# Scaling graph messages with the attention weight: 25 ScalarE activations per chunk for one VectorE product

## The chip, the cores and the metric

The kernel runs on one core of a Trainium2 chip. The metric is the device time of one execution in microseconds (us); the time before is the median of three runs. One further execution was recorded by the hardware profiler, and every duration below comes from it. PE is TensorE, DVE VectorE, ACT ScalarE, POOL GpSimd, SP the engine that issues most plain loads.

## What is computed

One graph attention layer over 12,500 nodes and 400,000 edges that are sorted by destination:

```python
xl = einsum('ni,nio->no', h, hetero_w[node_type]) + hetero_b[node_type]      # h = relu(layernorm(x))
alpha = lrelu(concat([xl[dst], xl[src], ete, eae]) @ att_w)                  # one score per edge
alpha = exp(alpha - amax[dst]);  alpha = alpha / (segment_sum(alpha, dst) + 1e-16)
msg = concat([xl[src], eae]) @ lin_w * alpha                                 # 32 numbers per edge
out = x + segment_sum(msg, dst)
```

The product `... * alpha` in the fourth line is what the change is about. The kernel does not know the final maximum and denominator while it passes over the edges; it multiplies each message by exp(score minus the running maximum) and carries 32 sums and the denominator along.

## The kernel before

**Tiling.** Each of the 128 partitions owns 3125 consecutive edges, cut into 125 chunks of T = 25 edges. A loop of 25 iterations holds 5 chunks each (u = 0 to 4, each with its own input buffers; the last iteration is written out after the loop). The message of an edge (before scaling) is a row of a node table gathered by source node plus a PE product of the edge attributes.

**Gathers.** POOL issues an indirect DMA for each column of 128 edges: 21, 22, 21, 22 and 21 per chunk in the five chunks (`gath[u]`, line 443), 2675 in all. The 3 or 4 remaining columns of a chunk are made by PE and DVE with one-hot products (lines 636, 949, 970, 976). POOL waits only for a chunk's index buffer `meta_sb[u]`, which SP reloads once the scan of the chunk five before is over. So POOL can run up to five chunks ahead.

**Order in one chunk.** DVE makes the picks of destination scores (line 983) and the one-hots (949, 997), then waits for the chunk's gathers and adds them to PE's product (lines 1048 and 1050, into `msg`). It works out the score, the running maximum and the exponents' arguments (to line 1072, `args_ready`). ACT makes the exponential (533, `exp_done`), copies two columns to the output rows (536, 537), and spreads the decay factors (540, `keep_ready`). DVE meanwhile copies the last sums (1078), the weights (1086) and makes the product of messages and weights (1087) into `terms`. `terms` is stored as 33 fields by 26 edge places, so that the scan along the edges (1094) can run over all fields in one instruction: consecutive fields of an edge lie 26 numbers apart. The scan needs `terms` and `keep`. After it ACT copies the sums to the output rows (546), issues their store, and begins the 50 sign activations of the next chunk (526, 528), which feed a count on PE (691). ACT then waits for the next arguments. `nc.scalar.mul` in `scale_attr` (518) is an activation too and already stands between exponential and signs in each chunk.

The chunk bodies of each engine are plain instruction sequences; counters (semaphores) order them across engines. `need(k, at)` and `step` are waits and increments of DVE's own counter.

Of the kernel before, what the change touches and what calls it, by code (L numbers as in the profile page):

```python
# [7 lines left out]
F_IN = 32  # L8
# [6 lines left out]
P = 128  # L15
# [3 lines left out]
T = 25  # L19
# [27 lines left out]
def gnn_kernel(nc, x, meta, dst_rows, dst_tmajor, sel_src, row_edges, row_last, edge_attr_t, node_type,  # L47
               hetero_wT, hetero_bT, edge_type_emb, edge_attr_w, att_w, lin_w, out):
    fp32, bf16, i32 = mybir.dt.float32, mybir.dt.bfloat16, mybir.dt.int32
    ALU, ACT, AX = mybir.AluOpType, mybir.ActivationFunctionType, mybir.AxisListType  # L50
# [13 lines left out]
    with ctx:  # L64
        def sb(name, shape, dt=fp32):
            return ctx.enter_context(nc.sbuf_tensor(name, shape, dt))

        def sem(name):
            return ctx.enter_context(nc.semaphore(name))
# [36 lines left out]
        def in_node_buf(at, shape, parts=P):  # L106

            size = shape[0] * shape[1]
            return node_buf[0:parts, at:at + size].rearrange("p (a b) -> p a b", b=shape[1])
# [36 lines left out]
        msg = in_node_buf(2 * TG * P, [T, VW])  # L146
# [3 lines left out]
        wts = sb("wts", [P, 2, T])  # L150
        terms = in_node_buf(2 * TG * P + T * VW, [VW, T + 1])
# [14 lines left out]
        def part_of(k, g):  # L166
            return parts[:, k, g, :].rearrange("p (f n) -> p f n", n=GN)
# [23 lines left out]
        scale = sb("scale", [P, 2, NPP])  # L191
# [79 lines left out]
        args_ready = sem("args_ready")  # L271
        exp_done = sem("exp_done")
        keep_ready = sem("keep_ready")
        sums_ready = sem("sums_ready")
        rows_sums = sem("rows_sums")
        head_idx_ready = sem("head_idx_ready")
# [37 lines left out]
        def count(n):  # L314

            return n + 1

        def selected(i, u):

            return i * TS_ITER + TS_BEFORE[u]  # L320

        def start_at_one(eng, *sems):
            for s in sems:
                eng.sem_inc(s, 1)

        def is_unsorted(eng):
            eng.wait_ge(unsorted_ready, 1)
            return eng.value_load(unsorted_i[0:1, 0:1], min_val=0, max_val=1)
# [153 lines left out]
        @block.scalar  # L482
        def _(act):
            start_at_one(act, hmT_sb, rows_sums, *stored)

            act.wait_ge(node_w_mm, 1)
            nc.scalar.copy(node_w[:], ps_misc[:, 0, 0:YW])
            nc.scalar.copy(node_b[:], ps_misc[0:MB, 0, YW:2 * YW]).then_inc(node_w_sb, 1)
            act.wait_ge(var_ready, 1)
            nc.scalar.sqrt(stat[:, 3, :], stat[:, 2, :]).then_inc(dev_ready, 1)  # L490
            with act.Fori(0, NODE_ITERS // 2) as i:
                for k in range(2):
                    n = i * 2 + k
                    act.wait_ge(hmT_mm, n + 1)
                    act.wait_ge(tab_mm, n + 1)
                    for b, w in enumerate((4 * P, 3 * P)):
                        last = nc.scalar.copy(hmT[k][:, b * 4 * P:b * 4 * P + w], ps_hmT[k][:, b, 0:w])
                    last.then_inc(hmT_sb, 1)

            act.wait_ge(tab_sb, NODE_ITERS + 2)  # L500
            for g in range(NG):
                nc.scalar.copy(part_of(0, g), table_group[g]).then_inc(part_copied, 1)
            for g in range(NG):
                act.wait_ge(rest_ready, g + 1)
                nc.scalar.copy(part_of(1, g), part_rest[g]).then_inc(part_copied, 1)
            for g in range(NG):
                act.wait_ge(rest_ready, NG + g + 1)
                last = nc.scalar.copy(part_of(2, g), part_rest[g])
            last.then_inc(parts_ready, 1)
            act.wait_ge(parts_ready, 1)  # L510
            act.wait_ge(head_counted, 1)
            act.wait_ge(table_out, 16)

            def scale_attr(c):

                act.wait_ge(attr_mm, c + 1)
                act.wait_ge(eae_ready, count(c))
                nc.scalar.mul(eae_s, ps_attr[0:G * F_EDGE, :, 0:TG * P // 2], SLOPE).then_inc(eae_scaled, 1)

            def chunk(i, u, final):  # L520
                c = i * U + u

                act.wait_ge(places_ready, c + 1)
                act.wait_ge(signs_mm, count(c))
                for t in range(T):
                    nc.scalar.activation(sign_hi[:, t, :], half128[:], ACT.Sign, bias=hic[u][:, t:t + 1],  # L526
                                         scale=-1.0)
                    last = nc.scalar.activation(sign_lo[:, t, :], half128[:, 0:NPP], ACT.Sign,  # L528
                                                bias=loc[u][:, t:t + 1], scale=-1.0)
                last.then_inc(signs_ready, 1)  # L530

                act.wait_ge(args_ready, c + 1)
                nc.scalar.activation(wts[:], args[:], ACT.Exp).then_inc(exp_done, 1)  # L533

                act.wait_ge(stored[u], i * 16 + 1)
                nc.scalar.copy(rows[u][:, :, VW], mrun[:, 1:T + 1])
                nc.scalar.copy(rows[u][:, :, VW + 1], dstc[u][:, 1:T + 1])
                act.wait_ge(exp_done, c + 1)
                act.wait_ge(sums_ready, count(c))
                nc.scalar.copy(keep[:, :, 1:T + 1], wts[:, 1:2, :].broadcast_to([P, VW, T])).then_inc(  # L540
                    keep_ready, 1)
                if not final:
                    scale_attr(c + 1)

                act.wait_ge(sums_ready, count(c + 1))
                nc.scalar.copy(rows[u][:, :, 0:VW], sums[:, :, 1:T + 1].rearrange("p f t -> p t f")).then_inc(  # L546
                    rows_sums, 1)
                act.wait_ge(rows_sums, count(c + 1))
                act.dma_start(rows_pm[:, ds(c * T, T), :], rows[u][:]).then_inc(stored[u], 16)

            scale_attr(0)
            with act.Fori(0, ITERS - 1) as i:
                for u in range(U):
                    chunk(i, u, False)
            for u in range(U):
                chunk(ITERS - 1, u, u == U - 1)

            flag = is_unsorted(act)
            with act.If(flag < 1):
                act.wait_ge(targs_ready, 1)  # L560
                nc.scalar.activation(wtail[:], mtail[:], ACT.Exp)
                nc.scalar.activation(fix[:, 2:3], fix[:, 1:2], ACT.Exp).then_inc(texp_done, 1)
            with act.If(flag >= 1):
                with act.Fori(0, EPP) as t:
                    act.wait_ge(merge_args, t + 1)
                    nc.scalar.activation(wtail[:], mtail[:], ACT.Exp)
                    nc.scalar.activation(fix[:, 2:3], fix[:, 1:2], ACT.Exp).then_inc(merge_exp, 1)
# [169 lines left out]
        def _(dve):  # L737
            v = nc.vector
# [11 lines left out]
            def step(ins):  # L750

                steps[0] += 1
                ins.then_inc(dve_step, 1)
                return steps[0]
# [218 lines left out]
            def take_sum(i, u, j):  # L973

                dve.wait_ge(sel_read, count(selected(i, u) + j + 1))
                return step(v.tensor_reduce(gath[u][:, T - 1 - j, 0:VW], sel_prod, AX.X, ALU.add))  # L976
# [23 lines left out]
            def chunk(i, u, at, final):  # L1000
                c = i * U + u
# [54 lines left out]
                k = step(v.tensor_tensor(alpha[:], msg[:, :, F_IN], escore[:], ALU.add))  # L1056
# [3 lines left out]
                k = step(v.scalar_tensor_tensor(alpha[:], alpha[:], SLOPE, alpha[:], ALU.mult, ALU.max))  # L1060
# [4 lines left out]
                k = step(v.tensor_tensor_scan(mrun[:, 1:T + 1], pen[:], alpha[:], mrun[:, 0:1], ALU.add, ALU.max))  # L1065
# [3 lines left out]
                k = step(v.tensor_tensor(args[:, 1, :], mrun[:, 0:T], pen[:], ALU.add))  # L1069
# [13 lines left out]
                if not final:  # L1083
                    place(3, *after, at)
                dve.wait_ge(exp_done, c + 1)
                v.tensor_copy(terms[:, F_IN, 1:T + 1], wts[:, 0, :])
                k = step(v.tensor_tensor(terms[:, 0:F_IN, 1:T + 1].rearrange("p f t -> p t f"), msg[:, :, 0:F_IN],  # L1087
                                         wts[:, 0, :].unsqueeze(2).broadcast_to([P, T, F_IN]), ALU.mult))
                if not final:
                    k_take = take_sum(*after, 2)  # L1090
                dve.wait_ge(keep_ready, c + 1)
                dve.wait_ge(rows_sums, count(c))
                need(k, at)
# [19 lines left out]
            with dve.Fori(0, ITERS - 1) as i:  # L1113
                for u in range(U):
                    chunk(i, u, i * STEPS, False)
            assert steps[0] == before + STEPS
            steps[0] = before + STEPS * (ITERS - 1)
            for u in range(U):
                chunk(ITERS - 1, u, 0, u == U - 1)
# [160 lines left out]
```

## Time and profile before

| | |
|---|---|
| median of the runs | 5777.1 us (5774.23 to 5807.59) |
| profiled execution, first to last instruction | 4081.6 us |
| VectorE busy in it | 2835.9 us |
| ScalarE busy in it | 2278.0 us |
| GpSimd busy in it | 3109.5 us |
| chunk loops, about | 160 to 3920 us of it |

The profiled execution's span is 1695.5 us shorter than the median of the runs; the profile shows nothing of what lies around the span. Times inside the span are read from the trace, times of the whole kernel from the runs. "Idle before" of a group is the time in which the engine stood still directly ahead of that group's instructions, with what it waited for; "issue" means that no other engine's work is seen as the cause.

### The profile page before, as it was taken

Reading aid. Unit: us, or ns where it says so; the run is one execution under the profiler, and the core shown is the slowest. Engines: PE = TensorE matmul, PEld = TensorE weight load, DVE = VectorE, ACT = ScalarE, POOL = GpSimd, SP = SyncE. Lnnn points to the kernel's source line nnn. Section 1 sums busy time; section 2 is a strip of 40 time slices with the busy share of each in tenths; the row PEclk is TensorE's granted clock in tenths of the full one; section 3 lists DMA queues with packets and bytes.
Section 4 is the critical chain, followed back from the end, with each engine's and each line's share of the span. In section 5 each row is a group of like instructions: output and inputs, shape, how many; then the busy total and the mean of one; then the engine's idle time right before and its main releaser. Section 6 shows DMA issues by size and latency. Waiting matters only on the chain.

```text
span 4081.6 us, 79224 instructions
## 1 busy us (share of the span) xinstructions
PE 3088.9 (76%) x24063; PEld 1924.5 (47%) x24063; DVE 2835.9 (69%) x12580; ACT 2278.0 (56%) x7080; POOL 3109.5 (76%) x2790
## 2 busy tenths in 40 slices
PE   5787877787787877887878877777877887887820
PEld 4454544444444544544544444444544554554510
DVE  6887776776776776776776776776776776776730
ACT  2466565565565565565565565565565565665620
POOL 1777777777777777777777777777777777777757
PEclk9899889888889898888898898999998889989865
DMA  3932232232232232232232232232232332322211
GB/s 99 103 76 64 62 78 62 62 79 62 62 79 62 63 78 62 63 78 62 62 78 62 63 78 62 62 79 62 65 76 62 69 73 62 77 64 62 43 35 29
DMA packets 188948, 273.63 MB, mean 67 GB/s; under 512 B 84416, under 2 KB 145232, under 8 KB 187616
## 3 DMA queue, kind: packets, MB, share of 16 engines
q1 hardware_dynamic: 81584, 162.45, 15.5%
q0 software_dynamic: 88800, 48.54, 10.5%
q10 hardware_dynamic: 18000, 56.01, 3.5%
q8 instruction: 246, 4.03, 0.4%
q14 instruction: 318, 2.61, 0.2%
HBM read 204.76 MB, written 62.01 MB: 65 GB/s over the span
## 4 chain that ended last, share of the span: by engine, by line
POOL 75%; issue 21%; PE 1%; DMA 1%; DVE 1%; SPq 0%; POOLq 0%; ACT 0%; ACTq 0%; DVEq 0%
POOL gath L443 73%; POOL node_buf L478 2%; PE ps_misc L603 1%; PE ps_misc L600 0%; DMA tails<-rows_dram 0%; DMA table_dram<-node_buf 0%; DMA rlast_i<-row_last_in 0%; PE ps_pick L612 0%; PE ps_attr L591 0%; DMA rows_dram<-rows 0%; DMA gath<-table_dram,meta 0%; PE ps_pick L591 0%; DVE sums L1094 0%; SPq L356 0%; ACT rows L546 0%
## 5 line engine op out<-in xcount | busy, mean ns | idle before, releaser
L443 POOL DMA_INDIRECT gath<-table_dram,meta x2675 | 3009.7, 1125 | 904.8 <-issue 904.5
L636 PE MATMUL ps_misc<-parts,dst_f 128*128 128x462 bf16 x9450 | 2011.1, 372 | 9.7 <-issue 6.4
L636 PEld LDWEIGHTS ps_misc<-parts,dst_f 128*128 128x128 bf16 x9450 | 935.1, 101 | 958.4 <-issue 147.6
L526 ACT ACTIVATE hi_f<-half,hic 128x128 bf16<-128x128 f32 x3125 | 1209.2, 387 | 61.7 <-ACT rows L546 61.4
L528 ACT ACTIVATE hi_f<-half,loc 128x98 bf16<-128x98 f32 x3125 | 1130.1, 362 | 0.0
L983 DVE SCALAR_TENSOR_TENSOR h<-free,loc,ps_pick 128x98 f32<-128x98 f32 x3125 | 778.6, 308 | 87.7 <-issue 87.0
L648 PE MATMUL ps_pick<-s_dst,onehot 128*128 128x98 bf16 x9375 | 539.0, 215 | 210.7 <-DVE h L983 151.1
L691 PE MATMUL ps_msg<-hi_f 128*128 128x98 bf16 x3125 | 244.0, 261 | 545.1 <-DVE node_buf L1050 545.1
L1048 DVE TENSOR_TENSOR node_buf<-gath,ps_msg 128x495 f32<-128x495 f32 x125 | 83.5, 668 | 818.6 <-DMA gath<-table_dram,meta 818.6
L648 PEld LDWEIGHTS ps_pick<-s_dst,onehot 128*128 128x128 bf16 x9375 | 485.6, 102 | 299.7 <-DVE h L983 193.5
L533 ACT ACTIVATE wts<-args 128x50 f32<-128x50 f32 x125 | 30.7, 245 | 926.2 <-DVE args L1072 926.1
L691 PEld LDWEIGHTS ps_msg<-hi_f 128*128 128x128 bf16 x3125 | 224.0, 129 | 591.8 <-issue 586.4
L546 ACT COPY rows<-sums 128x825 f32<-128x825 f32 x125 | 224.2, 1794 | 415.9 <-DVE sums L1094 415.9
L949 DVE TENSOR_SCALAR dst_f<-dst_f,part_group 128x128 bf16<-128x128 f16 x1750 | 353.6, 272 | 0.8 <-DMA dst_f<-sel_code_dram 0.7
L970 DVE TENSOR_TENSOR h<-ps_misc,sel_mask 128x462 f32<-128x462 f32 x450 | 283.9, 631 | 64.0 <-PE ps_misc L636 63.4
L976 DVE TENSOR_REDUCE gath<-h 128x33 f32<-128x462 f32 x450 | 281.6, 626 | 2.7
L983 DVE DVE_READ_ACCUMULATOR h<-free,loc,ps_pick 128x1 f32 x3125 | 247.0, 79 | 0.0
L1094 DVE TENSOR_TENSOR_SCAN sums<-keep,node_buf 128x858 f32<-128x858 f32 x125 | 242.0, 1936 | 0.1
L1087 DVE TENSOR_TENSOR node_buf<-node_buf,wts 128x800 f32<-128x800 f32 x125 | 209.7, 1677 | 0.0
L680 PEld LDWEIGHTS ps_msg<-msg_w,node_buf 80*128 80x128 f32 x1250 | 194.3, 196 | 26.1 <-issue 2.4
L680 PE MATMUL ps_msg<-msg_w,node_buf 80*128 80x165 f32 x1250 | 202.5, 310 | 0.0
L657 PE MATMUL ps_attr<-attr,attr_w 80*80 80x320 f32 x500 | 167.8, 460 | 4.4
(199 smaller groups left out, 1585.4 us busy)
## 6 DMA issues: line engine op xcount, KB each, us to landing
hib<-dst_hi_dram SPq DMA_DIRECT2D x125, 800.0 KB, 5.4
rows_dram<-rows ACTq DMA_DIRECT2D x125, 437.5 KB
gath<-table_dram,meta POOLq DMA_INDIRECT x2675
attr<-edge_attr_t_in SPq DMA_DIRECT2D x125, 200.0 KB, 6.2
dst_f<-sel_code_dram SPq DMA_DIRECT2D x125, 128.0 KB, 5.4
meta<-meta_in SPq DMA_DIRECT2D x125, 38.0 KB, 1.8
parts<-x_in SPq DMA_DIRECT2D x2, 1568.0 KB, 6.6
rows_dram<-tile_rows SPq DMA_DIRECT2D x1, 1715.0 KB
```

Source lines behind the costliest of these rows:

```text
L443: nc.gpsimd.indirect_dma_start(gath[u][:, t, :], None, table_dram, bass.IndirectOffsetOnAxis(ap=meta_sb[u][:, t:t + 1], axis=0)).then_inc( ...
L526: nc.scalar.activation(sign_hi[:, t, :], half128[:], ACT.Sign, bias=hic[u][:, t:t + 1], scale=-1.0)
L528: last = nc.scalar.activation(sign_lo[:, t, :], half128[:, 0:NPP], ACT.Sign, bias=loc[u][:, t:t + 1], scale=-1.0)
L636: last = nc.tensor.matmul(ps_sel[:, j % 2, 0:VW * GN], sel_onehot[:, g, j * P:(j + 1) * P], parts[:, k, g, :], start=(g == 0 and k == 0), ...
L648: last = nc.tensor.matmul(ps_pick[:, g % 2, j * NPP:(j + 1) * NPP], onehot[:, t * P:(t + 1) * P], s_dst[:, k, :], start=(k == 0), stop=(k ...
L680: last = nc.tensor.matmul(ps_msg[:, g // 3, g % 3 * G * VW:(g % 3 + 1) * G * VW], eae_flat[:, g * P:(g + 1) * P], msg_w[:], start=True, st ...
L691: last = nc.tensor.matmul(ps_signs, sign_hi[:, t, :], sign_lo[:, t, :], start=(t == 0), stop=(t == T - 1))
L949: last = v.tensor_scalar(sel_onehot[:, g, tiles], code_sb[u][:, tiles], part_group[:, g:g + 1], None, ALU.is_equal)
L970: v.tensor_tensor(sel_prod, ps_sel[:, j % 2, 0:VW * GN].rearrange("p (f n) -> p f n", n=GN), sel_mask[:, j:j + 1, :].broadcast_to([P, VW, ...
L976: return step(v.tensor_reduce(gath[u][:, T - 1 - j, 0:VW], sel_prod, AX.X, ALU.add))
L983: v.scalar_tensor_tensor(pick[:, t, :], free98[:], loc[u][:, t:t + 1], ps_pick[:, g % 2, j * NPP:(j + 1) * NPP], ALU.is_equal, ALU.mult, a ...
L1094: v.tensor_tensor_scan(sums[:].rearrange("p f t -> p (f t)"), keep[:].rearrange("p f t -> p (f t)"), terms.rearrange("p f t -> p (f t)"), ...
```

## The change

After the exponential, ACT makes 25 activations, one per edge place t. Each copies the 32 message numbers of that edge in each partition, `msg[:, t, 0:32]`, into field-major `terms[:, 0:32, t+1]`, with the weight `wts[:, 0, t:t+1]` as per-partition scale. The last one raises a new semaphore `terms_ready`. They stand ahead of the copy to `keep`. DVE's product is gone; its copy of the weights into the 33rd field stays. The scan waits for `terms_ready` too.

```diff
+        terms_ready = sem("terms_ready")
@@ scalar engine, chunk()
                 act.wait_ge(exp_done, c + 1)
                 act.wait_ge(sums_ready, count(c))
+                for t in range(T):
+                    last = nc.scalar.activation(terms[:, 0:F_IN, t + 1], msg[:, t, 0:F_IN], ACT.Copy,
+                                                scale=wts[:, 0, t:t + 1])
+                last.then_inc(terms_ready, 1)
                 nc.scalar.copy(keep[:, :, 1:T + 1], wts[:, 1:2, :].broadcast_to([P, VW, T])).then_inc(
                     keep_ready, 1)
@@ vector engine, chunk()
                 dve.wait_ge(exp_done, c + 1)
-                v.tensor_copy(terms[:, F_IN, 1:T + 1], wts[:, 0, :])
-                k = step(v.tensor_tensor(terms[:, 0:F_IN, 1:T + 1].rearrange("p f t -> p t f"), msg[:, :, 0:F_IN],
-                                         wts[:, 0, :].unsqueeze(2).broadcast_to([P, T, F_IN]), ALU.mult))
+                k = step(v.tensor_copy(terms[:, F_IN, 1:T + 1], wts[:, 0, :]))
                 if not final:
                     k_take = take_sum(*after, 2)
+                dve.wait_ge(terms_ready, c + 1)
                 dve.wait_ge(keep_ready, c + 1)
```

## Rows read from the trace of the kernel before

**Rows 1.** The page: span, and busy time of each engine (share, instructions)

```profile
span 4081.6 us, 79224 instructions
PE 3088.9 (76%) x24063; PEld 1924.5 (47%) x24063; DVE 2835.9 (69%) x12580; ACT 2278.0 (56%) x7080; POOL 3109.5 (76%) x2790
```

**Rows 2.** The page: the chain that ended last, share of the span by engine

```profile
POOL 75%; issue 21%; PE 1%; DMA 1%; DVE 1%; SPq 0%; POOLq 0%; ACT 0%; ACTq 0%; DVEq 0%
```

**Rows 3.** Groups by line and shape: count | busy us, mean ns | idle before, releaser

```profile
L443 POOL DMA_INDIRECT gath<-table_dram,meta x2675 | 3009.7, 1125 | 904.8 <-issue 904.5 <-DMA rows_dram<-rows 0.3
L528 ACT ACTIVATE hi_f<-half,loc 128x98 bf16<-128x98 f32 x3125 | 1130.1, 362 | 0.0
...
L1094 DVE TENSOR_TENSOR_SCAN sums<-keep,node_buf 128x858 f32<-128x858 f32 x125 | 242.0, 1936 | 0.1
L546 ACT COPY rows<-sums 128x825 f32<-128x825 f32 x125 | 224.2, 1794 | 415.9 <-DVE sums L1094 415.9
...
L1087 DVE TENSOR_TENSOR node_buf<-node_buf,wts 128x800 f32<-128x800 f32 x125 | 209.7, 1677 | 0.0
...
L540 ACT COPY keep<-wts 128x825 f32<-128x825 f32 x125 | 109.8, 879 | 0.0
...
L1048 DVE TENSOR_TENSOR node_buf<-gath,ps_msg 128x495 f32<-128x495 f32 x125 | 83.5, 668 | 818.6 <-DMA gath<-table_dram,meta 818.6
...
L526 ACT ACT_TABLE_LOAD x24 | 30.8, 1283 | 154.7 <-issue 154.6
...
L536 ACT COPY rows<-mrun 128x25 f32<-128x25 f32 x125 | 27.4, 219 | 0.0
```

**Rows 4.** Timeline of one chunk: start us, us, engine, line [idle before]

```profile
2001.58 0.67 DVE L1048 TENSOR_TENSOR node_buf<-gath,ps_msg 128x495 f32<-128x495 f32 x1 [7.30 <-DMA gath<-table_dram,meta]
...
2004.87 0.24 ACT L533 ACTIVATE wts<-args 128x50 f32<-128x50 f32 x1 [6.96 <-DVE args L1072]
...
2005.23 0.88 ACT L540 COPY keep<-wts 128x825 f32<-128x825 f32 x1
...
2005.96 1.66 DVE L1087 TENSOR_TENSOR node_buf<-node_buf,wts 128x800 f32<-128x800 f32 x1
...
2006.66 1.64 POOL L443 DMA_INDIRECT gath<-table_dram,meta  x1 [0.31 <-issue]
...
2007.97 1.94 DVE L1094 TENSOR_TENSOR_SCAN sums<-keep,node_buf 128x858 f32<-128x858 f32 x1
2008.60 2.07 POOL L443 DMA_INDIRECT gath<-table_dram,meta  x1 [0.30 <-issue]
...
2010.97 0.94 POOL L443 DMA_INDIRECT gath<-table_dram,meta  x1 [0.30 <-issue]
...
2012.67 0.36 ACT L528 ACTIVATE hi_f<-half,loc 128x98 bf16<-128x98 f32 x1
...
2012.93 0.39 ACT L526 ACTIVATE hi_f<-half,hic 128x128 bf16<-128x128 f32 x1
```

**Rows 5.** Timeline of VectorE: line 1048 in five consecutive chunks

```profile
3223.47 0.67 DVE L1048 TENSOR_TENSOR node_buf<-gath,ps_msg 128x495 f32<-128x495 f32 x1 [8.47 <-DMA gath<-table_dram,meta]
...
3253.51 0.67 DVE L1048 TENSOR_TENSOR node_buf<-gath,ps_msg 128x495 f32<-128x495 f32 x1 [7.30 <-DMA gath<-table_dram,meta]
...
3284.44 0.67 DVE L1048 TENSOR_TENSOR node_buf<-gath,ps_msg 128x495 f32<-128x495 f32 x1 [9.76 <-DMA gath<-table_dram,meta]
...
3313.83 0.67 DVE L1048 TENSOR_TENSOR node_buf<-gath,ps_msg 128x495 f32<-128x495 f32 x1 [6.04 <-DMA gath<-table_dram,meta]
...
3344.07 0.66 DVE L1048 TENSOR_TENSOR node_buf<-gath,ps_msg 128x495 f32<-128x495 f32 x1
```

**Rows 6.** Timeline of GpSimd: first and last gather that begins while line 1087 runs

```profile
166.55 1.32 POOL L443 DMA_INDIRECT gath<-table_dram,meta  x1 [0.30 <-issue]
...
3895.52 1.34 POOL L443 DMA_INDIRECT gath<-table_dram,meta  x1 [0.30 <-issue]
```

**Rows 7.** Line 443 by source: duration ns min/median/max

```profile
L443 POOL DMA_INDIRECT gath<-table_dram,meta x2675: 940/945/6056, 92.7 to 3916.3; - x192
```

## The prediction, made before the change was run

> **What bounds the kernel now.** I read four views, in this order. The busy times: POOL and PE stand at 76% each, DVE at 69% and ACT at 56%, so no engine is full and the shares decide nothing [rows 1]. The chain that ended last: 75% of the span is POOL and 21% "issue" [rows 2]. The groups: line 443 is busy 3009.7 us in 2675 gathers, and nearly all of its idle time (904.5 us, 0.34 us a gather) is issue, so POOL hardly ever waits for another engine [rows 3]. The timeline then shows the consumer: DVE stands 7.30 us before line 1048 until the last gather has landed, and ACT stands 6.96 us before the exponential, behind DVE [rows 4]. The reader is to see that POOL issues one gather after another for the whole loop, and that DVE and ACT follow with some time to spare.
>
> How much to spare matters here. Over five consecutive chunks DVE waits 8.47, 7.30, 9.76, 6.04 and 0 us, 31.6 us in all, 6.3 us a chunk [rows 5]. The chunk without a wait is the one at the turn of the loop; its lateness is made up in the chunk after it. Line 1048 waits 818.6 us in all [rows 3], or 6.5 us a chunk.
>
> The second thing to see is what a gather costs on POOL. The median is 945 ns but the mean 1125 ns [rows 7, 3], so 2675 gathers carry about 480 us that the shortest ones do not need. The timeline shows where some of it falls. The gather begun at 2006.66, while DVE runs line 1087 (2005.96 to 7.62), takes 1.64 us and ends 0.68 us after the product does. The gather begun at 2008.60, while the scan of line 1094 runs until 9.91, takes 2.07 us and ends 0.76 us after the scan; the next takes 0.94 us [rows 4]. Of the 125 products, 124 have one such gather; the first takes 1.32 and the last 1.34 us [rows 6], and all of them together take 97.8 us more than 0.945 us each. So DVE's product holds up the engine that sets the time.
>
> **What is removed.** DVE loses 1677 ns a chunk, 209.7 us in all [rows 3]. As DVE waits for gathers, that alone is worth nothing. What it is worth lies on POOL: 124 gathers no longer wait for it, 98 us (0.79 each).
>
> One rule speaks against this gain. The trace has gathers waiting for a product of two SBUF operands [rows 4]. The Trainium skill, "SBUF — State Buffer", section "Who interferes with whom", says that such a tensor_tensor takes only the read side of the port pair that GpSimd shares, and infers that descriptor generation needs the write side, so that it would not be stalled; but the same list says that a VectorE instruction with two SBUF inputs contends with a GpSimd one that reads SBUF, and a gather reads its indices there. By the first sentence the gain would be nothing, by the second the 98 us stand.
>
> **What is added.** 25 activations of 32 numbers with one per-partition operand. The nearest row is line 528: 98 numbers, one per-partition operand (there a bias), 362 ns; line 526 with 128 numbers takes 387 ns or so (0.39 in the timeline), 0.83 ns a number. For 32 numbers this gives 362 - 66 x 0.83 = 307 ns. They overlap: line 526 starts 0.26 us after line 528, which takes 0.36 [rows 4], so 0.10 us is shared. That leaves 0.21 us per instruction, 5.35 us a chunk. Bounds: all 307 ns without overlap, 7.7 us; or dearer by the scattered write. A scattered read of 825 numbers costs 1794 ns where an ordered one costs 879 ns (lines 546 and 540), 1.1 ns a number, which would be 35 ns an instruction or 0.9 us a chunk; but line 536, which writes 25 numbers to places 35 apart, takes only 219 ns [rows 3], so I take the write as free. The change puts no table load into a chunk if the copy belongs to the functions in use: line 518 is already such an activation, and only 24 table loads are seen in 125 chunks [rows 3].
>
> **How the chain of a chunk moves.** Now the scan starts 6.39 us after line 1048 (2001.58 to 7.97), with `keep` made from 2005.23 to 6.11 and waiting for the product [rows 4]. Afterwards the 25 activations take the place of the `keep` copy at 2005.23, 3.65 us after line 1048, and the copy comes behind them. The scan starts at 3.65 + 5.35 + 0.88 + 0.05 = 9.93 us. So the chain is D = 3.5 us longer (3.2 to 6.0 between the bounds, 4.4 with a dear write). Behind DVE's longer wait for `terms_ready` and `keep_ready` are queued the scan, the one-hot products of a fourth column, and the whole next chunk; SP's reloads of meta, hib, code and attr wait for the scan, but these serve the chunk five later, whose gathers begin some 120 us (four chunks of 30) afterwards. On ACT the copy to the output rows, its store, and the next signs wait for the scan and shift by the same D; ACT's 6.96 us before the exponential shrink by D too, and PE's sign products, which wait for DVE's line 1050, have the same room.
>
> **Is it hidden?** Five chunks need 5 x 3.5 = 17.5 us of the 31.6 us of waits, and POOL's gain takes 5 x 0.8 = 4 us more from them: 10 us are left. The chunk at the turn of the loop gets its D late, and the next, with 8.47 us, takes both (7.0) [rows 5]. So the added time costs nothing while the gathers run. The cover is gone when 5D + 4 passes 31.6, at D = 5.5, which is 0.29 us per activation. Only the last chunk has no gathers behind it: there D is paid once, 4 us.
>
> **What is unknown in size.** The gathers run in a rhythm of 1.245 us that is fixed to line 1048, since that line starts when the last of them lands. Shifting the scan, the one-hots (949, 997) by 3.5 us lands them on other places in this rhythm. A gather caught by the scan loses anything from 0.4 to 1.65 us; it is 1.13 us now (2.07 - 0.94), and the middle of the two is 1.0. For the scan at 9.93 us a gather would begin at about 10.03, right at the edge between the two ends. I take no net change, with 0.6 us a chunk, 75 us, either way.
>
> **The sum.** 0 (DVE's time) - 98 (gathers freed) + 0 (activations, hidden) + 4 (the last chunk) = -94 us: the profiled span would go from 4081.6 to 3988 us. The 1695.5 us between span and median are in no view; I take them as unchanged, and so 5777.1 - 94 = 5683 us.
>
> **Rivals.** (a) The gain is given back. The freed gathers meet the later scan and one-hots at worse places, or they were held by something else than the product. For: POOL's lost time is 480 us of which the product makes only 98; the scan alone makes 139 by the same count. Against: the two rows of blocked gathers end at fixed distances from the DVE instructions [rows 4]. Price: between -20 and +4 us, 5757 to 5781, no change.
> (b) ScalarE becomes the bound; slower. One mechanism: the activation costs 0.40 us instead of 0.21, for example through the pairing of scattered write and per-partition scale that no row shows. Then D = 25 x 0.40 - 1.81 = 8.2 us, five chunks need 41 us where 31.6 are there, 9.4 us an iteration are lost, 235 us in 25 iterations: 6012 us. It decides from 0.325 us an activation (5D = 31.6); at 0.307, no overlap, half of the gain would be lost, about 5730. Against: 0.21 follows from two rows of the same engine. For: the Trainium skill, "ScalarE: Activation LUTs", "Rules for kernel authors", gives plain multiplications to VectorE. Its cost formula in "What ACT_TABLE_LOAD costs" (about 280 ns + 0.833 ns a number with one pointer operand, 93 ns overlap) gives 214 ns here, and the trace agrees (307 - 95).
> (c) The activation needs its own table: two loads of 1283 ns in each chunk [rows 3]. D becomes 6.1 us, 5D = 30.5: cover just used up, the gain about half gone, 5730.
>
> **How the numbers follow.** Forecast, gathers freed and activations hidden: 0.52, with its own range from 5610 (94 + 75 us gained) to 5757. Rival (a): 0.28. Rival (b): 0.15. Rival (c) 0.05. The predicted time is 5683 us. The range has to reach over (a) and (c), and leaves out (b) and a little of the forecast's tail: 5620 to 5795. A run of this kernel can tell about 1% from no change, that is 58 us. Faster by more: most of the forecast (gain above 58 us), 0.50. Within 1%: (a), the weak end of the forecast and half of (c), 0.33. Slower: (b) and the bad end of phase, 0.17.
>
> **What would show it.** In the changed kernel's profile: 3125 activations of 128x32 with some 307 ns each, starting 0.21 us apart; line 443's mean down from 1125 to about 1090 ns, and no gather of 1.3 to 1.7 us ahead of the scan; the wait before line 1048 down from 818.6 us to about 300; the scan 9.9 us after line 1048; DVE busy about 2630 us, ACT about 3200. Wrong if the mean of line 443 stays, if line 1048 no longer waits (then ACT or DVE is the bound), or if the runs move otherwise than the span, since their 1695 us are not in it.

## The result and the profile after

The changed kernel is slower: 6192.13 us median of 4 runs (6166.32 to 6196.37) against 5775.66 us for the kernel before (5763.42 to 5807.59), a ratio of 1.071 with a 95% interval of 1.067 to 1.076. The forecast was 5683 us, faster.

Its profile shows another condition than the one that [rows 1 to 7] show. From the page of the changed kernel, the head, the granted clock of PE in tenths over 40 slices, and the chain that ended last:

```profile
span 6193.3 us, 82229 instructions
PE 3737.0 (60%) x24063; PEld 2101.4 (34%) x24063; DVE 2678.9 (43%) x12455; ACT 2982.5 (48%) x10205; POOL 2795.4 (45%) x2790
PEclk8677777777777777777777777777777777777785
issue 33%; PE 26%; another core or an unknown queue 18%; DVE 14%; ACT 6%; POOL 2%; DMA 0%; DVEq 0%; SPq 0%; ACTq 0%; POOLq 0%
```

The span is 6193.3 us, three microseconds below the time of its run (6196.4). For the kernel before the span was 1695 us below the median [rows 1]. POOL, which carried 75% of the chain [rows 2], now carries 2%; a third of the chain is "issue", time in which an engine waits for nothing that the profile shows. The waits tell whose (engine and line, what for, us in total, times, longest):

```profile
POOL gath L444 <- DMA meta<-meta_in: 2349.7, 117, 45.2
ACT wts L534 <- DVE args L1077: 2039.0, 99, 126.1
...
PE ps_pick L653 <- issue: 878.7, 691, 4.1
...
PE ps_misc L641 <- issue: 450.4, 472, 6.0
...
DVE sums L1098 <- ACT node_buf L542: 368.2, 96, 5.2
PE ps_msg L696 <- issue: 347.2, 326, 2.6
```

GpSimd stands 2350 us waiting for its index buffers, so it has run five chunks ahead and has nothing to do; before, it never waited ([rows 3]: 904.5 us of issue is its own rhythm). PE has some 1750 us of issue idle in its four largest rows (three are shown; line 685 adds 71.6). The timeline of PE shows what that is (start us, us, engine, line, count, idle before):

```profile
3018.28 1.26 PE L662 MATMUL ps_attr<-attr,attr_w 80*80 80x320 f32 x4
3019.38 1.56 PE L685 MATMUL ps_msg<-msg_w,node_buf 80*128 80x165 f32 x10
...
3025.13 0.21 PE L653 MATMUL ps_pick<-s_dst,onehot 128*128 128x98 bf16 x1 [1.18 <-issue]
...
3031.47 0.54 PE L641 MATMUL ps_misc<-parts,dst_f 128*128 128x462 bf16 x1 [0.86 <-issue]
3033.58 0.54 PE L641 MATMUL ps_misc<-parts,dst_f 128*128 128x462 bf16 x1 [1.57 <-issue]
3034.97 0.54 PE L641 MATMUL ps_misc<-parts,dst_f 128*128 128x462 bf16 x1 [0.85 <-issue]
...
3042.67 8.66 PE L641 MATMUL ps_misc<-parts,dst_f 128*128 128x462 bf16 x33 [0.16 <-issue]
```

From 3021 to 3042 us PE mostly starts one matmul each 1.4 us, then it makes 33 in 8.66 us. The profile sees no operand that is late. I call this crawling, and count as a stretch of it a row of matmuls that start 0.6 to 4 us apart, at least five times on end. There are 112 stretches in this trace, 1639 us from their first to their last start, and not one in the trace of [rows 4]. That PE lacks instructions while it crawls is the reading that fits it; no row proves it. Two other causes do not fit. The DMA engines are 12% busy in those 21 us, with 16 gathers, so it is not a full DMA. The granted clock is lower in them (0.62, against 0.77 in the 8.6 us that follow), but a matmul of line 641 takes 0.54 us there and PE then stands for 0.85 us or more, which is no slower matmul. Nor do the stretches end as the "instruction" transfers of queue 8 (16 KB each) arrive: of the 112, none ends in the 2.5 us behind the start of one, and the one shown ends 11.6 us behind it.

The block of activations that I had forecast for one chunk is there all the same (timeline of ScalarE and VectorE in the changed kernel):

```profile
3000.70 0.24 ACT L534 ACTIVATE wts<-args 128x50 f32<-128x50 f32 x1 [18.93 <-DVE args L1077]
...
3001.06 5.44 ACT L542 ACTIVATE node_buf<-node_buf,wts 128x32 f32<-128x32 f32 x25
3006.37 0.86 ACT L545 COPY keep<-wts 128x825 f32<-128x825 f32 x1
...
3007.41 1.95 DVE L1098 TENSOR_TENSOR_SCAN sums<-keep,node_buf 128x858 f32<-128x858 f32 x1 [5.17 <-ACT node_buf L542]
```

The 25 activations take 5.31 us to the start of the copy (0.212 each), and DVE stands 5.17 us for them.

### The profile page after: what moved, and what is told of

Read it like the earlier page. It is cut to its first block, busy times and chain, and to the rows that moved or that the text cites. A ratio compares the mean times of both kernels' runs of the same rounds, so it can differ in the third digit from the quotient of the medians.

```text
span 6193.3 us, 82229 instructions
## 1 busy us (share of the span) xinstructions
PE 3737.0 (60%) x24063; PEld 2101.4 (34%) x24063; DVE 2678.9 (43%) x12455; ACT 2982.5 (48%) x10205; POOL 2795.4 (45%) x2790
## 4 chain that ended last, share of the span: by engine, by line
issue 33%; PE 26%; another core or an unknown queue 18%; DVE 14%; ACT 6%; POOL 2%; DMA 0%; DVEq 0%; SPq 0%; ACTq 0%; POOLq 0%
PE ps_misc L641 15%; DVE h L988 5%; PE ps_pick L653 5%; ACT node_buf L542 4%; DVE dst_f L954 2%; PE ps_msg L685 2%; PE ps_attr L662 2%; POOL node_buf L479 2%; PE ps_msg L696 1%; DVE h L975 1%; DVE node_buf L1024 1%; ACT hi_f L527 0%; DVE gath L981 0%; ACT hi_f L529 0%
## 5 line engine op out<-in xcount | busy, mean ns | idle before, releaser
L444 POOL DMA_INDIRECT gath<-table_dram,meta x2675 | 2695.7, 1008 | 3217.4 <-DMA meta<-meta_in 2349.7
L641 PE MATMUL ps_misc<-parts,dst_f 128*128 128x462 bf16 x9450 | 2352.4, 405 | 555.1 <-issue 450.4
L641 PEld LDWEIGHTS ps_misc<-parts,dst_f 128*128 128x128 bf16 x9450 | 988.3, 107 | 1792.9 <-issue 1065.3
L653 PE MATMUL ps_pick<-s_dst,onehot 128*128 128x98 bf16 x9375 | 696.3, 225 | 1231.8 <-issue 878.7
L653 PEld LDWEIGHTS ps_pick<-s_dst,onehot 128*128 128x128 bf16 x9375 | 547.9, 107 | 1416.2 <-issue 986.9
L542 ACT ACTIVATE node_buf<-node_buf,wts 128x32 f32<-128x32 f32 x3125 | 688.6, 340 | 31.4 <-issue 31.2
L696 PE MATMUL ps_msg<-hi_f 128*128 128x98 bf16 x3125 | 242.3, 223 | 354.2 <-issue 347.2
L685 PE MATMUL ps_msg<-msg_w,node_buf 80*128 80x165 f32 x1250 | 300.1, 394 | 72.0 <-issue 71.6
L685 PEld LDWEIGHTS ps_msg<-msg_w,node_buf 80*128 80x128 f32 x1250 | 274.9, 261 | 120.8 <-issue 107.4
L662 PE MATMUL ps_attr<-attr,attr_w 80*80 80x320 f32 x500 | 232.3, 599 | 17.2 <-issue 14.1
L1002 DVE TENSOR_SCALAR onehot<-hib,part 128x3200 bf16<-128x3200 bf16 x125 | 131.6, 1053 | 0.0
```

The costliest lines, as they stand in the source:

```text
L444: nc.gpsimd.indirect_dma_start(gath[u][:, t, :], None, table_dram, bass.IndirectOffsetOnAxis(ap=meta_sb[u][:, t:t + 1], axis=0)).then_inc( ...
L542: last = nc.scalar.activation(terms[:, 0:F_IN, t + 1], msg[:, t, 0:F_IN], ACT.Copy, scale=wts[:, 0, t:t + 1])
L641: last = nc.tensor.matmul(ps_sel[:, j % 2, 0:VW * GN], sel_onehot[:, g, j * P:(j + 1) * P], parts[:, k, g, :], start=(g == 0 and k == 0), ...
L653: last = nc.tensor.matmul(ps_pick[:, g % 2, j * NPP:(j + 1) * NPP], onehot[:, t * P:(t + 1) * P], s_dst[:, k, :], start=(k == 0), stop=(k ...
L662: last = nc.tensor.matmul(ps_attr[0:G * F_EDGE, b, 0:TG * P // 2], attr_w[:], attr_sb[u][:, b * (TG * P // 2):(b + 1) * (TG * P // 2)], st ...
L685: last = nc.tensor.matmul(ps_msg[:, g // 3, g % 3 * G * VW:(g % 3 + 1) * G * VW], eae_flat[:, g * P:(g + 1) * P], msg_w[:], start=True, st ...
```

## The experiments

Each series ran on one chip with the kernel before beside it. The series fell on chips of two kinds. On three (numbers 0, 4, 8) the kernel before takes 4087 to 4106 us, on two (7, 9) it takes 5724 to 5874 us. The tables that follow say which. Chip 7 was met twice and was alike both times, each other chip once, and the chip of the first profile and of the result is not on record. So "kind of chip" stands for what each series found: whether it is the chip or something about it at that time, no run tells.

### Was the first profile like the runs?

e1_before is the kernel before, unchanged.

> The kernel before, unchanged, profiled once more. Theory A (the recorded execution of before was not like its timed runs, and the missing 1695 us lie inside the loop): the span is near 5770 us, POOL waits for the index buffers and PE shows idle time put down to issue, as in the changed kernel. Theory B (my prediction's assumption: the 1695 us lie around the span and the loop is bound by gathers): the span is again near 4082 us while the runs take 5775 us.

It ran on chip 4: 4086.6 us (8 runs), with a profiled execution of 4111.6 us whose span is 4109.7 us. So nothing of 1695 us lies around the span (1.9 us do here); the median of the runs and the first profile came from different conditions. Neither theory as written was right on that chip: A's time was wrong, B's span was right and its explanation wrong.

e11_before, the same file, met chip 7.

> The kernel before once more, to have its profile in the slower condition if this series meets it. Theory A: near 5750 us its profile shows some 1700 us of PE idle time put down to issue, GpSimd waiting for index buffers (about 1900 us) and no wait ahead of line 1048; near 4100 us it repeats the first profile.

5895.7 us, beside 5874.4 us for the runs of before, ratio 1.006 (1.000 to 1.011). Its waits:

```profile
POOL gath L443 <- DMA meta<-meta_in: 2016.0, 110, 45.6
ACT wts L533 <- DVE args L1072: 1727.1, 75, 113.6
...
PE ps_pick L648 <- issue: 726.5, 631, 6.4
...
PE ps_msg L691 <- issue: 508.2, 462, 3.3
...
PE ps_misc L636 <- issue: 280.3, 241, 29.0
PE ps_msg L680 <- issue: 240.7, 231, 2.4
```

Theory A holds. PE's issue idle is 726.5 + 508.2 + 280.3 + 240.7 = 1756 us here and 878.7 + 450.4 + 347.2 + 71.6 = 1748 us in the changed kernel; over all of PE's lines it is 1918 us here and 1782 us there (1895 us in e17_after). PE crawls about as long with the change as without it. The 7% are not more crawling.

### The changed kernel on the other kind of chip

e5_after is the changed kernel, unchanged, on chip 8; e10_after the same on chip 9; e13_after on chip 0; e17_after on chip 7.

> The changed kernel, unchanged, timed and profiled beside the kernel before at a second time. The kernel before took 4087 us in the first series of experiments and 5776 us beside the changed kernel. Theory A (two conditions of the chip: in one PE is starved of instructions and the chain is bare, in the other gathers bound the loop as in the first profile): if before takes about 4087 us again, the changed kernel takes about 4000 us, 2% less, with line 1048's successor waiting for gathers; if before takes about 5775 us, it takes about 6190 us. Rival B (the changed kernel brings the starving about by itself, for example through its longer ACT program): PE's idle time put down to issue is large and the time near 6190 us while before takes 4087 us beside it.

> The changed kernel once more, to pair it with before wherever this series runs. Theory A: 3968 us where before takes about 4100 us; about 6190 us where before takes about 5775 us; the two conditions never within one series.

> The changed kernel, the yardstick of this series for the three that follow. Where before takes 5700 to 5900 us: 6150 to 6200 us. Where before takes about 4100 us: 3968 us.

> The changed kernel beside e18_both and before, in the hope of a chip on which PE is starved. There: 6150 to 6200 us, 5 to 8% over before. Where gathers bound the loop: 3.2% less than before, for the third time.

| chip | before, us | changed, us | ratio (95%) |
|---|---|---|---|
| 8 (e5_after) | 4105.9 | 3968.3 | 0.967 (0.965 to 0.969) |
| 0 (e13_after) | 4104.6 | 3977.1 | 0.968 (0.965 to 0.971) |
| 9 (e10_after) | 5724.2 | 6194.1 | 1.077 (1.067 to 1.087) |
| 7 (e17_after) | 5769.4 | 6177.2 | 1.072 (1.066 to 1.079) |

Theory A again, and rival B (the change itself brings the crawling about) falls: the kernel before crawls as well on chips 7 and 9, the changed one not on 0 and 8. The same edit is worth 3.2 to 3.3% less or 7.2 to 7.7% more, by the chip. e5_after's groups, which stand against [rows 3]:

```profile
L444 POOL DMA_INDIRECT gath<-table_dram,meta x2675 | 2890.2, 1080 | 902.7 <-issue 902.3 <-DMA rows_dram<-rows 0.3
L641 PE MATMUL ps_misc<-parts,dst_f 128*128 128x462 bf16 x9450 | 2030.3, 375 | 142.0 <-DVE h L975 134.1 <-issue 6.0 <-DVE dst_f L954 1.5
L542 ACT ACTIVATE node_buf<-node_buf,wts 128x32 f32<-128x32 f32 x3125 | 679.5, 340 | 0.0
L1098 DVE TENSOR_TENSOR_SCAN sums<-keep,node_buf 128x858 f32<-128x858 f32 x125 | 244.0, 1952 | 554.3 <-ACT node_buf L542 527.7 <-ACT keep L545 26.5
L1053 DVE TENSOR_TENSOR node_buf<-gath,ps_msg 128x495 f32<-128x495 f32 x125 | 83.3, 667 | 251.9 <-DMA gath<-table_dram,meta 251.9
```

The gather's mean falls from 1125 ns [rows 3] to 1080 ns: 2675 x 45 ns = 120 us of the 138 us gained (the 1125 ns are of the first profile; the kernel before was not traced on chip 8). The wait ahead of the addition shrinks from 818.6 us to 251.9 us and is still there, so the activations are hidden. And this is what a chunk's gathers look like there, beside the scan (timeline):

```profile
2006.37 0.94 POOL L444 DMA_INDIRECT gath<-table_dram,meta  x1 [0.30 <-issue]
2007.62 0.94 POOL L444 DMA_INDIRECT gath<-table_dram,meta  x1 [0.31 <-issue]
...
2011.36 0.94 POOL L444 DMA_INDIRECT gath<-table_dram,meta  x1 [0.30 <-issue]
2011.43 1.95 DVE L1098 TENSOR_TENSOR_SCAN sums<-keep,node_buf 128x858 f32<-128x858 f32 x1 [5.12 <-ACT node_buf L542]
2012.61 1.52 POOL L444 DMA_INDIRECT gath<-table_dram,meta  x1 [0.31 <-issue]
```

The gather of 1.64 us that stood behind the product [rows 4] is gone. The gather before the scan gets away 0.07 us ahead of it and the next is caught late, so that it takes 1.52 us instead of 2.07.

With this the gain can be added up, gather by gather. What all gathers take beyond 945 ns each falls from 482 us in the first profile to 362 us here, by 119 us. Those that begin in the product lost 98 us, and these are gone. Those that begin in the scan lose 110 us instead of 139, another 29 us gained; the remaining gathers lose 8 us more than they did.

### The two halves of the change

e2_no_product and e14_no_product leave out VectorE's product (so 32 of 33 fields of the sums are not the layer's) and put nothing in its place:

```diff
-                v.tensor_copy(terms[:, F_IN, 1:T + 1], wts[:, 0, :])
-                k = step(v.tensor_tensor(terms[:, 0:F_IN, 1:T + 1].rearrange("p f t -> p t f"), msg[:, :, 0:F_IN],
-                                         wts[:, 0, :].unsqueeze(2).broadcast_to([P, T, F_IN]), ALU.mult))
+                k = step(v.tensor_copy(terms[:, F_IN, 1:T + 1], wts[:, 0, :]))
```

> The kernel before with DVE's product of messages and weights left out and nothing in its place (terms keeps old numbers in 32 of its 33 fields, so the output is not the layer's). Theory A (the chain from the score to the scan is bare): the scan starts 1.5 us earlier in each of 125 chunks, about 190 us less, 5590 us. Theory B (gathers set the time, the product costs only what it holds up on GpSimd): 98 us less, 5680 us. If neither the chain nor GpSimd bounds the loop: 5775 us.

> The kernel before without VectorE's product and with nothing in its place (32 of the 33 fields of terms keep old numbers). Earlier it took 1.6% less where gathers bound the loop. Where PE is starved: theory A (time there follows the chain from the addition to the scan) says 1.5 us less in each chunk that is bare, between 60 us (42 of 125 chunks) and 190 us (all of them) less than before. Rival (what hurts there is that VectorE's product is missing): more time than before.

e12_both, e15_both and e18_both keep the product and make the 25 activations too, into a tensor of their own:

```diff
                 act.wait_ge(sums_ready, count(c))
+                for t in range(T):
+                    nc.scalar.activation(extra[:, :, t], msg[:, t, 0:F_IN], ACT.Copy,
+                                         scale=wts[:, 0, t:t + 1])
                 nc.scalar.copy(keep[:, :, 1:T + 1], ...
```

> The kernel before with its VectorE product kept, and the 25 activations made as well, ahead of the copy to keep, into a tensor that nobody reads. The scan starts as late as in the changed kernel (10.0 us after the addition instead of 6.3), but the product still stands on VectorE. It parts the two halves of the change. Theory A on a chip where gathers bound the loop: the activations are hidden and the gain is gone, 4090 to 4110 us, the time of before within 1%, and the mean gather stays near 1.13 us. Theory A on a chip where PE is starved of instructions (before near 5725 to 5775 us): the longer chain alone costs what the change costs, 6190 us. Rival there: if what hurts is something the product's removal does, the time stays below 5850 us.

> Before with its product kept and the 25 activations added. Where PE is starved, theory A: the same time as the changed kernel of this series within 1%, since the scan starts equally late; the earlier 3.9% over before would then belong to that chip, and the changed kernel would show 4% there too. Rival (the chain is only half of the 7%): 3% less than the changed kernel. Where gathers bound the loop: the time of before within 1%, and so 3% more than the changed kernel.

> Product kept and activations added. Where PE is starved, theory A (the chain alone): within 1% of e17_after. Rival (the chain is half of it, the rest comes with taking the product from VectorE): 2 to 4% less than e17_after. Where gathers bound the loop: 0.4% less than before, as last time.

| | chip 4 | chip 0 | chip 7, first | chip 7, second |
|---|---|---|---|---|
| before | 4087.4 | 4104.6 | 5874.4 | 5769.4 |
| no product | 4021.7, 0.984 (0.981 to 0.986) | 4047.9, 0.986 (0.984 to 0.988) | | |
| product and activations | | 4088.4, 0.996 (0.995 to 0.998) | 6113.2, 1.039 (1.032 to 1.045) | 6089.4, 1.056 (1.051 to 1.062) |
| changed kernel | | 3977.1, 0.968 | | 6177.2, 1.072 |

Where gathers bound the loop, taking the product away gives 57 to 66 us. Adding the activations costs nothing: the scan starts 10 us after the addition in e15_both, VectorE's wait for gathers falls from 866.6 (e14_no_product) to 384.6 us, and the time does not rise. It falls by 16 us, and the gathers don't tell why: their mean is 1124 ns, as in the first profile. The two halves alone make 57 + 16 = 73 us, together they make 127 us. Much of the rest is the place of the scan among the gathers, which each variant sets anew: the gathers that begin in it lose 139 us in the first profile, 133 in e15_both, 181 and 182 in e2_no_product and e14_no_product, and 110 and 113 in e5_after and e13_after. So without the product 98 us are freed and some 43 us of them go to the scan, which now starts 4.8 us after the addition; the longer chain of the activations moves it to a better place. Rival (a) of the prediction names this, and where the product alone is taken away it comes true in part.

On chip 7 the same activations, with the product still on VectorE, cost 320 us of the changed kernel's 408 us in one series (6089.4 - 5769.4, 6177.2 - 5769.4). So the longer chain is most of the loss, 78% in this series. In the first series on chip 7 the activations cost 239 us (6113.2 - 5874.4), with no changed kernel beside them, so the share is rough. Theory A asked for all of the loss, within 1%; the difference of 88 us is 1.4% and the intervals do not touch. Some fifth of the loss comes with the absence of the product, and no run shows how: the kernel without the product did not run on a chip of this kind.

### Dose

e3_half and e16_half give VectorE 13 places and ScalarE 12:

```diff
+ON_DVE = 13
@@ scalar engine
-                for t in range(T):
+                for t in range(ON_DVE, T):
                     last = nc.scalar.activation(terms[:, 0:F_IN, t + 1], msg[:, t, 0:F_IN], ACT.Copy,
@@ vector engine
-                k = step(v.tensor_copy(terms[:, F_IN, 1:T + 1], wts[:, 0, :]))
+                v.tensor_copy(terms[:, F_IN, 1:T + 1], wts[:, 0, :])
+                k = step(v.tensor_tensor(terms[:, 0:F_IN, 1:ON_DVE + 1].rearrange("p f t -> p t f"),
+                                         msg[:, 0:ON_DVE, 0:F_IN],
+                                         wts[:, 0, 0:ON_DVE].unsqueeze(2).broadcast_to([P, ON_DVE, F_IN]), ALU.mult))
```

> The changed kernel with the work shared: DVE makes the product for 13 of the 25 edge places, ACT the activations for the other 12, at the same time. The scan should start 3.65 + 12 x 0.21 + 0.88 + 0.05 = 7.1 us after the addition of line 1048, against 6.4 before and 10.1 in the changed kernel. Theory A (bare chain): 0.7 us x 125 = 90 us more than before, 5865 us. Rival (the 7% come from something that goes with having many more ACT instructions or from ACT being fuller, not from the chain): 12 of 25 parts of 417 us, 5975 us.

> Half and half: 13 places on VectorE, 12 on ScalarE, the scan 7.25 us after the addition. Where PE is starved, theory A: 0.9 us of the changed kernel's 3.7 us, a quarter of its loss, 60 to 120 us more than before. Rival (the loss goes with the number of activations): half of its loss, 210 to 240 us more. Where gathers bound the loop: 1.4% less than before again.

4035.1 us on chip 4, ratio 0.986 (0.983 to 0.988), and 4058.7 us on chip 0, ratio 0.989 (0.988 to 0.991). The gathers that begin in the shorter product lose only 6 to 7 us, those in the scan 174 to 178 us. Both expectations of the first text were made for a bare chain and do not apply there; of the second text the last sentence does (1.1% less, not 1.4%). No chip of the other kind was met, so the dose is not measured where it would have told most.

e4_double makes 50 activations a chunk, 25 of them into `extra`, ahead of the real ones:

```diff
+                for t in range(T):
+                    nc.scalar.activation(extra[:, :, t], msg[:, t, 0:F_IN], ACT.Copy,
+                                         scale=wts[:, 0, t:t + 1])
                 for t in range(T):
                     last = nc.scalar.activation(terms[:, 0:F_IN, t + 1], msg[:, t, 0:F_IN], ACT.Copy,
```

> The changed kernel with 25 more activations of the same kind per chunk ahead of the real ones, written to a tensor that nobody reads. Theory A (bare chain): 25 x 0.21 = 5.3 us more per chunk, 663 us more than the changed kernel, 6855 us. Theory B (part of it still hidden): clearly less than 663 us more.

4384.8 us on chip 4, ratio 1.072 (1.070 to 1.075). Here the cover is gone, as the groups say:

```profile
L445 POOL DMA_INDIRECT gath<-table_dram,meta x2675 | 2825.1, 1056 | 1272.7 <-issue 875.8 <-DMA meta<-meta_in 397.0
L1102 DVE TENSOR_TENSOR_SCAN sums<-keep,node_buf 128x858 f32<-128x858 f32 x125 | 243.4, 1947 | 1123.6 <-ACT node_buf L546 1078.2 <-ACT keep L549 45.4
L1057 DVE TENSOR_TENSOR node_buf<-gath,ps_msg 128x495 f32<-128x495 f32 x125 | 82.3, 659 | 0.0
```

VectorE no longer waits for a gather and GpSimd waits 397 us for index buffers. The scan starts 15.6 us after the addition (median), 9.3 us later than before. Five chunks then need 46 us where 31.6 are to be had [rows 5], 15 us an iteration and 375 us in 25 iterations; 297 us are measured. So the budget of the prediction is right to about a quarter, and the edge lies between one and two sets of activations.

### A load on PE in place of the crawl

e6_fewer_pe takes two of the three bf16 parts of the table out of the selections (the selected rows are less exact). e7_before_pe and e8_after_pe repeat the selections of columns 1 and 2 three times in the kernel before and in the changed one:

```diff
 e6:
-                    for k in range(3):
+                    for k in range(1):
 e7, e8:
+REPS = (1, 3, 3, 1)
-                for g in range(NG):
-                    for k in range(3):
+                for g, k in [(g, k) for _ in range(REPS[min(j, 3)]) for g in range(NG) for k in range(3)]:
```

> The kernel before with 7 instead of 21 products per one-hot selection (only the first of the three bf16 parts of the table, so the selected rows are less exact): 6300 of PE's 24063 matmuls and as many weight loads gone. If gathers bound the loop (before near 4087 us): no change beyond 1%. If PE is starved of instructions (before near 5775 us): each missing pair saves about 1.4 us of the starved stretches, several hundred us less.

> The kernel before with PE made the laggard: the one-hot selections of columns 1 and 2 are worked out three times over (same result), 84 more matmuls a chunk, placed where the profile of the slower condition shows PE behind. Expected near 4087 + 125 x (84 x 0.2 us - room of PE of some 6 us) = 5400 us, with line 1048 no longer waiting for gathers and GpSimd waiting for its index buffers. It is the yardstick for the next kernel.

> The changed kernel with the same 84 extra matmuls a chunk. Theory A (the sign of the change hangs on what bounds the loop; once it is not the gathers, the 3.7 us by which the scan starts later are paid in each chunk): 3.7 x 125 = 460 us more than the kernel before with the same load. Theory B (a load on PE hides the longer chain as well, and the 7% need the starving of instructions itself): about the same time as it, or less.

e6_fewer_pe took 4100.6 us on chip 8, ratio 1.000 (0.999 to 1.001): with 6300 matmuls fewer nothing moves where gathers bound the loop. Its mean granted clock is 0.76, against 0.88 in the first profile and 0.73 to 0.75 on the crawling chips, so a low mean clock goes with a fast run too. e7_before_pe and e8_after_pe met chip 9, where PE crawls anyway: 7290.3 and 7249.6 us, 1.259 (1.244 to 1.275) and 1.256 (1.245 to 1.268) of before. With that load the change costs nothing, theory B's side. The waits fit this: VectorE stands 2577 us for PE's selections in e7_before_pe (line 970 for 636) and 2603 us in e8_after_pe, and the scan starts 34 and 30 us after the addition (medians), much later than the activations alone would put it. So PE's work covers their chain. The added load was not like the crawl, and the experiment tells no more about the crawl than this: a longer ACT chain also disappears under PE, if PE is behind at that place.

### A version for both

e9_share7 gives ScalarE only 7 places, behind the copy to `keep`:

```diff
-ON_DVE = 13
+ON_DVE = 18
@@ scalar engine: the copy to keep now ahead of the activations
+                nc.scalar.copy(keep[:, :, 1:T + 1], wts[:, 1:2, :].broadcast_to([P, VW, T])).then_inc(
+                    keep_ready, 1)
                 for t in range(ON_DVE, T):
```

> A version meant to beat both in either condition: DVE makes the product for 18 edge places, ACT the activations for 7, behind the copy to keep. The scan should start 6.1 to 6.4 us after the addition, as before or 0.3 us earlier, and the product on DVE takes 1.2 instead of 1.68 us. Where gathers bound the loop: 30 to 60 us less than before (4087 or 4106 there). Where the chain is bare (before near 5775): 0 to 40 us less.

On chip 9: 5788.6 us, ratio 1.011 (1.007 to 1.016). The kernel is 1% slower, where 0 to 40 us less were expected. The scan starts as early as 6.15 us after the addition, as designed, but only in few chunks (16 of 125 stay under 7 us): the median is 9.8 us, against 9.4 in e11_before on chip 7. In most chunks there the start of the scan is not set by the length of this chain alone, and why the version loses stays open. It met no chip of the other kind, and the half-and-half version none of this kind, so no version is known to beat both kernels on both.

## Why the prediction was wrong

**The step that failed** is in the sum: "The 1695.5 us between span and median are in no view; I take them as unchanged". They were no constant around the loop. They lie inside it, in the execution of a chip where PE crawls (e11_before: 5894.9 of 5898.0 us are span), and what they are decides the sign. The term that this made wrong is "+ 0 (activations, hidden)": in place of 0 the changed kernel loses 408 to 470 us there. The first paragraph's conclusion, that POOL issues one gather after another for the whole loop, is true for the profiled execution and false for the runs that were to be predicted. With a median 42% above the span of its own profile, "DVE and ACT follow with some time to spare" was not known for the runs. My last paragraph named this ("since their 1695 us are not in it") and gave it no chance of its own.

**Point by point, against a chip like the one in the first profile.** Gathers freed: 98 us forecast; 57 and 66 us measured for the removal alone, 127 and 138 us for the whole change. The term was right in kind and the sum on the low side (94 us). Phase of the scan: taken as zero, within 75 us; it was 29 us to the good with the change and 43 us to the bad with the removal alone. Activations hidden: forecast 0 us, measured -16 us (e15_both). Size of the block: 5.35 us forecast (25 x 0.21 is 5.25, a slip without weight), 5.31 us measured; 340 ns for one activation instead of 307, but they still start 0.21 us apart. ScalarE busy "about 3200" us, measured 2937 in e5_after. Scan 9.93 us after the addition forecast, 10.0 us measured. VectorE's wait "to about 300" us, measured 251.9; mean gather 1090 ns, measured 1080. Table loads, rival (c): none.

**Rival (b)** named the right side with the wrong cause. It asked for activations of 0.40 us; they cost 0.21 us. The loss came because the cover was not there: on the chips that crawl, VectorE waits 0 us for gathers (e11_before has no such wait in its rows, GpSimd waits 2016 us for its index buffers instead). The whole D, paid in every chunk, would be 3.7 x 125 = 463 us; measured were 408 to 470 us. The trace shows that it is not paid so evenly. On chip 7, of 115 chunks in the middle of the loop, 42 of e11_before take less than 33 us from one addition to the next, 23.9 us each, and 44 of e17_after, with 27.3 us each: 3.4 us more. The others take 57.1 and 59.0 us, 2 us more. Even in the short chunks the scan starts 9.2 us after the addition in e11_before and 11.4 us in e17_after (medians), 2.2 us later and not 3.7. So D is right as the size of what is bare, but how it turns into the loss is shown only in part.

**The rule against the gain**, that a product of two SBUF operands would not stall descriptor generation, is answered for this kernel: 124 of 125 products had a gather that began in them and ended 0.67 us (median) after them, 98 us in all, and e2_no_product, without them, takes 66 us less. The other sentence of the Trainium skill, "SBUF — State Buffer", section "Who interferes with whom", that a VectorE instruction with two SBUF inputs contends with a GpSimd one that reads SBUF, is the one that the traces agree with.

## What to carry to other kernels

Before costing anything, set the span of the profile against the median of the runs. If they differ by much more than the executions of one kernel do among themselves, the profile is of another condition than the runs (in every profiled execution here whose own time is known, the span is 2 to 3 us below it). Then ask for each cover that you use ("hidden behind the gathers") whether it exists in both, and give the case that it doesn't a rival with its own price, here simply D times the number of chunks. A change that moves work onto the chain between two engines is a bet on slack. A change that shortens what holds up the bounding engine pays only where that engine bounds, and part of it can go to the next thing that holds it up (43 of 98 us here). The split of the two halves into kernels of their own shows which is which.

## What the runs showed of the hardware

- Chips differ. The same program takes 4087 to 4106 us on chips 0, 4 and 8 and 5724 to 5874 us on 7 and 9. On the latter PE starts mostly one matmul each 1.4 us in 112 to 129 stretches, 1.6 to 1.8 ms in all, whether or not the change is made (with the load added on PE, 78 and 80 stretches, 1.0 ms), while the DMA engines are nearly idle (12% in the stretch shown). ScalarE has a little of it too: line 528 has 113 us of issue idle in e11_before and none in [rows 3]. What starves the engines there wasn't found.
- A VectorE product of two SBUF operands, and the scan, hold up a gather that GpSimd begins while they run until 0.67 and 0.75 us after their end (medians). 124 of 125 products and 124 of 125 scans did. Where GpSimd bounds the kernel, such an instruction has a price of its own, 0.79 us a piece for 1.68 us of VectorE.
- A ScalarE activation that writes 32 numbers 104 bytes apart takes 340 ns, 33 ns more than estimated from lines that write in order, and the next still starts 0.21 us later. That the scattered write makes the 33 ns was not tried by itself.
